# Eight fused layers on one core: the order of 1,112 steps from a table in place of a rule of turns

## The chip, the core and the metric

One core of a Trainium2 chip runs the whole program in one launch. Five instruction streams run side by side: TensorE (PE, with its weight loads PEld), VectorE (DVE), ScalarE (ACT), GpSimd (POOL) and SyncE (SP, which only issues DMAs here). Each executes its own instructions strictly in the order in which the program writes them, and they meet at semaphores. The metric is the device time of one execution in microseconds.

## The reference

A batch of 8 sequences of 256 tokens, 128 wide, goes through four attention layers and four feed-forward layers in turn. Each adds to `x` (arguments abridged, comments added):

```python
x = x + _L0_xattn_ref(_layernorm(x), ctx_1024, ...)  # L0x: gated retention, 16 heads
x = x + _L0_ffn_ref(_layernorm(x), ...)              # L0f: 8 experts, top 2, GELU
x = x + _L1_xattn_ref(_layernorm(x), ctx_1024, ...)  # L1x: bidirectional attention flow
x = x + _L1_ffn_ref(_layernorm(x), ...)              # L1f: shared + 7 experts, top 1, SwiGLU
x = x + _L2_xattn_ref(_layernorm(x), ctx_1024, ...)  # L2x: 16 heads, masked softmax
x = x + _L2_ffn_ref(_layernorm(x), ...)              # L2f: quantised, with a width-3 convolution
x = x + _L3_xattn_ref(ctx_1024, _layernorm(x), ...)  # L3x: 8 heads, 512 keys, normed q and k
x = x + _L3_ffn_ref(_layernorm(x), ...)              # L3f: 2 groups of 32 experts, top 2, SwiGLU
```

The mixture layers (L0f, L1f, L3f) choose experts by token, so rows are sent to DRAM by expert, read back in blocks, multiplied, stored and fetched again.

## The kernel before, in words

`x` stays in on-chip memory. Every layer is cut into units over the batch: L0x 4, L0f 2, L1x 8, L1f 2, L2x 8, L2f 8, L3x 8, L3f 4. A unit of a layer needs only the same tokens of the layer before, so units of neighbouring layers overlap, at most two of one layer. A unit is written as up to six generators (`on_pe`, `on_dve`, `on_act`, `on_pool`, `on_sync`), one an engine, each cut by `yield` into the same number of steps. L2x.5.11 below means layer L2x, unit 5, step 11 (counted from 0). One step of a unit stands on every engine at the same place of the list of steps; `stepwise` walks that list once for each engine and lets the generator of that unit emit its next piece. So the list alone sets the order of work inside every in-order stream. A "+L1x" entry is the place at which SP issues the weight loads of a layer.

The list has 1,112 entries. In the kernel before it is made by `tensor_program`, a rule of turns: the active units take turns in the order of layers; each time round a unit gains the credit of its layer in `STEPS` (0.8 to 1.7) and gives a step for each whole credit; a unit starts when the layer before has finished its tokens and the memory slabs that it needs are free (`SLABS`), and the second unit of a layer keeps a distance to the first.

Steps that the prediction speaks of, with the lines of the profile:

- L0f: `turn`, `up`, `down` of an expert block, one each step from step 15 on (L786, L795, L804, L806), GELU on ACT (L903), DVE copies (L850). L1x.0: transposes of the normed tokens (L362) and first product (L1426). `normalise` (L249 to L282) is a layer norm on DVE, `moments` (L303, L306) only its statistics, with the root on POOL (L315 to L332).
- L2x: steps 5 to 8 give scores to PSUM, which DVE reduces (L1791); steps 11 and 13 transpose the maxima (L1676), steps 14 to 18 are scores again and products (L1702, L1689), Exp on ACT (L1858); step 0 of a unit projects the context (L1628 to L1638).
- L2f: steps 5 to 8 are three matmuls each (L1972, L1974, L1976), with SiLU on ACT (L2103); step 10 transposes (L1987), DVE quantises (L2068 to L2075), and step 12 transposes its result (L1996).
- L3x: DVE step 0 is `moments` (with the one-time `set_up`, L2338 to L2343, in unit 0), step 2 writes the normed tokens (L2377), PE transposes them in step 3 (L2201); step 11 waits on DVE for key and query norms whose roots POOL makes (L2523, then L249 to L267) and scales (L2356); steps 15 to 18 turn heads and give scores, of which DVE takes maxima to step 22 (L2399); steps 24 to 32 are scores and products (PE L2272, Exp on ACT L2498, L2502), step 36 is the output product (L2325), after which DVE norms it.
- L3f: DVE step 0 is `normalise` of 4 tiles; steps 17 to 30 are 12 chunks, one a step: transposes of rows (L2711), up (L2734), down (L2747), SiLU on ACT (L2944), a DVE product (L2883); rows come by SP (L2615, stores L2623, weights L2633).

PSUM banks are given out in a ring of eight by `Banks.take` in the order of PE's steps; the next taker waits until the reader of the last use is done.

Of the kernel before, what the change touches and what calls it, by code (L numbers as in the profile page):

```python
# [146 lines left out]
def build(nc, ins, out):  # L147
    ctx = ExitStack()
    with ctx:
# [2855 lines left out]

        def tensor_program():

            uses = {n: set("".join(SLABS[n])) | set("" if n[1] == "3" else "G") for n in LAYERS}  # L3010
            started, finished, asked = dict.fromkeys(LAYERS, 0), dict.fromkeys(LAYERS, 0), []
            given = dict.fromkeys(LAYERS, 0)
            active, order = [], []
            ahead, apart = {(n, u): 0 for n in LAYERS for u in range(UNITS[n])}, {}

            def vacant(name, slabs):
                return not any(uses[n] & set(slabs) and finished[n] < UNITS[n] for n in LAYERS[:LAYERS.index(name)])

            def ask():
                while len(asked) < len(LAYERS) and vacant(LAYERS[len(asked)], SLABS[LAYERS[len(asked)]][0]):  # L3020
                    order.append(("load", LAYERS[len(asked)]))
                    asked.append(LAYERS[len(asked)])

            def start():
                for k, n in reversed(list(enumerate(LAYERS))):
                    mine = [a for a in active if a[1] == n]
                    if (n in asked and started[n] < UNITS[n] and len(mine) < 2
                            and vacant(n, SLABS[n][1] + (SLABS[n][2] if started[n] else ""))
                            and all(a[2] for a in mine)
                            and (k == 0 or given[LAYERS[k - 1]] * UNITS[n]  # L3030
                                 >= (started[n] + 1) * UNITS[LAYERS[k - 1]] * PARTS[LAYERS[k - 1]])):
                        active.append([made[n][1](started[n]), n, False, 0.0, started[n]])
                        started[n] += 1
                        return True
                return False

            ask()
            while start() or active:
                active.sort(key=lambda a: LAYERS.index(a[1]))
                for entry in list(active):  # L3040
                    unit, n, second, _, u = entry
                    before = next((a for a in active if a[1] == n and a[4] < u), None)
                    if second and entry is not next(a for a in active if a[1] == n):
                        continue
                    entry[3] += STEPS[n]
                    while entry[3] > 0.999:
                        if before in active and ahead[n, u - 1] - ahead[n, u] < apart[n]:
                            entry[3] = 0.0
                            break
                        if entry[2] and not vacant(n, SLABS[n][2]):  # L3050
                            break
# [182 lines left out]
```

## Time and profile before

| | us |
|---|---|
| median of three runs | 1491.45 (1487.0 to 1491.95) |
| span of the profiled execution | 1483.4 |
| PE busy in that span | 1185.0 (80%) |
| DVE, ACT, POOL busy | 802.1, 673.0, 433.6 |

The profile gives the profiled execution's time as its span, from the first instruction to the last. Nothing else of its own time is recorded, and the runs' median is 8.05 us above the span. A row's idle time stands before the named instruction, with what released it. PEclk is the share of full clock granted to PE.

### The profile page before, as it was taken

How to read it: one execution, taken by the hardware profiler on the slowest of the kernel's cores; microseconds unless marked ns; L12 is line 12 of the kernel's file. 1: busy time of each engine (PE TensorE's matmuls, PEld its weight loads, DVE VectorE, ACT ScalarE, POOL GpSimd, SP SyncE). 2: the span in 40 equal slices, each digit the busy share in tenths (PEclk: the TensorE clock that was granted, in tenths of full speed). 3: DMA queues.
4: the chain of work that ended last, by engine and by line, in shares of the span. 5: the costliest groups of instructions: out<-in, count | busy, mean ns of one | idle time of the engine just before them, and what ended most of it. 6: DMA issues, size and time to landing. Idle time of an engine off the chain costs nothing. (4 is left out here: it accounts for less than half of the span.)

```text
span 1483.4 us, 28125 instructions
## 1 busy us (share of the span) xinstructions
PE 1185.0 (80%) x10844; PEld 919.1 (62%) x10844; DVE 802.1 (54%) x2259; ACT 673.0 (45%) x1373; POOL 433.6 (29%) x822
## 2 busy tenths in 40 slices
PE   6776865987876899876878968969988997899453
PEld 4555865875875678554545755747764776578343
DVE  6676304436646345577557456485358535761722
ACT  1222544752442554543554735534754475447121
POOL 2214232005412311223261221216051515142234
PEclk9887997988996999898988989989997999899777
DMA  9002874535530324200000270004520452055165
GB/s 270 3 2 94 250 259 130 173 108 175 182 107 4 125 91 144 74 1 1 1 1 1 108 237 0 4 6 132 144 66 10 137 141 59 11 161 143 29 205 165
DMA packets 141144, 146.62 MB, mean 99 GB/s; under 512 B 13395, under 2 KB 125011, under 8 KB 140371
## 3 DMA queue, kind: packets, MB, share of 16 engines
q1 hardware_dynamic: 133842, 130.13, 28.6%
q0 software_dynamic: 7168, 14.69, 3.1%
q8 instruction: 86, 1.41, 0.4%
q14 instruction: 48, 0.39, 0.1%
HBM read 107.69 MB, written 37.09 MB: 98 GB/s over the span
## 5 line engine op out<-in xcount | busy, mean ns | idle before, releaser
L315 POOL TENSOR_SCALAR rsq_v<-moment 128x2 f32<-128x2 f32 (+1 forms) x26 | 6.2, 239 | 322.7 <-DVE moment L306 319.1
L2964 POOL DMA_INDIRECT L3f_rows<-xn,slabG x64 | 63.6, 993 | 119.6 <-DVE slabG L2841 101.7
L2399 DVE TENSOR_REDUCE slabB<-bank 128x1 f32<-128x512 f32 x128 | 78.6, 680 | 8.5 <-PE bank L2244 8.5
L1791 DVE TENSOR_REDUCE slabA<-bank 128x2 f32<-128x512 f32 x128 | 78.4, 682 | 4.1 <-PE bank L1663 4.0
L2883 DVE TENSOR_TENSOR slabG<-bank,slabG 128x256 f32<-128x256 f32 x48 | 20.2, 422 | 108.2 <-ACT slabG L2944 108.2
L1858 ACT ACTIVATE slabE<-bank 128x512 f32<-128x512 f32 x112 | 58.0, 618 | 34.9 <-PE bank L1702 34.7
L2272 PE MATMUL bank<-slabB,slabW 128*128 128x128 f32 x512 | 69.7, 281 | 0.0
L2383 DVE TENSOR_REDUCE slabW<-slabC 128x8 f32<-128x512 f32 x48 | 32.4, 680 | 65.9 <-ACT slabC L2462 65.8
L1074 POOL DMA_INDIRECT slabA<-L0f_made,slabA x32 | 30.8, 961 | 123.9 <-DMA L0f_made<-slabA 114.8
L2272 PEld LDWEIGHTS bank<-slabB,slabW 128*128 128x128 f32 x512 | 61.9, 192 | 8.2 <-issue 7.8
L903 ACT ACTIVATE slabA<-bank,slabA 128x128 f32<-128x128 f32 x184 | 52.7, 375 | 22.6 <-PE bank L795 21.7
L1702 PE MATMUL bank<-slabA 32*128 32x256 f32 x512 | 48.4, 448 | 13.2 <-DVE slabC L2071 10.0
L1226 PE MATMUL bank<-slabC,slabB 128*128 128x128 f32 x448 | 56.5, 281 | 1.6 <-ACT slabC L1351 1.2
L795 PE MATMUL bank<-slabA 128*128 128x128 f32 x368 | 52.5, 289 | 5.0 <-DMA slabA<-e_w_dram 3.7
L2211 PE MATMUL bank<-slabB,slabW 128*128 128x512 f32 x96 | 56.1, 670 | 0.4 <-DVE slabA L1801 0.3
L2462 ACT ACTIVATE slabC<-bank 128x512 f32<-128x512 f32 x48 | 28.8, 601 | 59.4 <-PE bank L2211 44.7
L1226 PEld LDWEIGHTS bank<-slabC,slabB 128*128 128x128 f32 x448 | 53.9, 197 | 2.5 <-ACT slabC L1351 1.7
L850 DVE COPY slabA<-bank 128x128 f32<-128x128 f32 x46 | 13.3, 290 | 73.8 <-PE bank L806 53.4
L2931 ACT ACTIVATE slabG<-bank 128x512 f32<-128x512 f32 x48 | 29.0, 604 | 52.6 <-PE bank L2711 52.4
L795 PEld LDWEIGHTS bank<-slabA 128*128 128x128 f32 x368 | 48.4, 205 | 7.2 <-issue 6.5
L2980 POOL DMA_INDIRECT slabC<-L3f_made,slabG x32 | 30.6, 957 | 70.4 <-DMA L3f_made<-slabC 61.7
L2711 PE MATMUL bank<-ident,slabE 128*128 128x128 f32 x192 | 31.5, 290 | 23.4 <-DMA slabE<-L3f_rows 23.4
(469 smaller groups left out, 3382.3 us busy)
## 6 DMA issues: line engine op xcount, KB each, us to landing
slabA<-e_w_dram SPq DMA_DIRECT2D x46, 578.0 KB, 4.3
slabB<-e_w_dram SPq DMA_DIRECT2D x28, 768.0 KB, 4.4
slabE<-L3f_rows SPq DMA_DIRECT2D x48, 256.0 KB, 3.5
L3f_made<-slabC SPq DMA_DIRECT2D x48, 256.0 KB, 2.5
slabD<-e_w_dram SPq DMA_DIRECT2D x64, 128.0 KB
ctxT<-e_w_dram SPq DMA_DIRECT2D x64, 128.0 KB
L3f_rows<-slabG SPq DMA_DIRECT2D x4, 1536.0 KB, 18.3
L0f_rows<-slabG SPq DMA_DIRECT2D x2, 1472.0 KB, 10.2
```

Source lines behind the costliest of these rows:

```text
L795: m = T.matmul(k.ap[:, tile_cols(c)], w1(n, c), rowsT[n % 2], start=True, stop=True, skip_group_check=True)
L903: A.activation(hb[n % 2][:, tile_cols(c)], k.ap[:, tile_cols(c)], ACT.Gelu, bias=b1(n, c)).then_inc(*(act.tell(*k.read) if c == FB - 1 els ...
L1226: m = T.matmul(k.ap[:, tile_cols(c)], w[:, j, tile_cols(c)], rowsT[n % 2], start=True, stop=True, skip_group_check=True)
L1702: m = T.matmul(bs[j].ap[:, kt * S:(kt + 1) * S], z["KT"][r, c, tile_cols(kt)], z["QT"][r, c, :], start=True, stop=True, skip_group_check=True)
L1791: V.tensor_reduce(nmx[:, :, c, 32 * j + HD:32 * j + HD + 1], b.ap.rearrange("p (i s) -> p i s", i=2), AX.X, ALU.max, negate=True).then_inc ...
L1858: A.activation(probs[(4 * c + j) % 8], b.ap, ACT.Exp).then_inc(*act.tell(*b.read))
L2211: T.matmul(b.ap, kvT[:, tok], Wk if kind == "kn" else Wq, start=True, stop=True, skip_group_check=True).then_inc(b.full[0])
L2272: m = T.matmul(obs[i].ap[:, tile_cols(h % 4)], p.ap[:, j * S + i * P:j * S + (i + 1) * P], Vv[:, ((2 * half + j) * H + h) * (HD + 1):((2 * ...
L2383: V.reduce_sum(norms[:, 8 * n:8 * n + 8], by_head(sqs[n % 2]), AX.X).then_inc(*dve.tell(sem("l3x_norms"), 6 * u + n + 1))
L2399: V.tensor_reduce(nmx[:, i, 64 * e + k:64 * e + k + 1], b.ap, AX.X, ALU.max, negate=True).then_inc(*dve.tell(*b.read))
L2711: t = T.transpose(b.ap[:, tile_cols(j)], rowsb[m % 3][:, j, :], ident)
L2964: G.indirect_dma_start(sent[u % 2][r], bass.IndirectOffsetOnAxis(ap=to[u % 2][:, k, 2 * t + r:2 * t + r + 1].bitcast(U32), axis=0), xn[:, ...
```

## The change

The credits, the slab rules and the rule of turns are gone. `TURNS`, a table written out by hand or by a program, lists the same 1,112 entries in another order; `turns` unpacks it and `tensor_program` only walks it. No instruction is added, removed or resized in the source. Of the 1,104 steps, 232 stand at the same place among the steps as before, 829 have moved by up to ten places and 43 by 11 to 17. The first 38 steps and the last ones from the last L3x unit's end (all of L3f.3) stand as before. The loads move too: +L1x from entry 2 to 11, +L1f 78 to 87, +L2x 212 to 220, +L2f 213 to 242, +L3x 384 to 383, +L3f 617 to 630. Line numbers after the table are 48 higher.

```diff
+TURNS = """
++L0x +L0f L0x.0*8 L0x.1 +L1x L0x.0 L0x.1 L0x.0 L0x.1 L0x.0 L0x.1 L0x.0 L0x.1 L0x.0 L0x.1 L0x.0 L0x.1 L0x.0
...
-        SLABS = {"L0x": ("B", "CE", ""), "L0f": ("A", "", ""), "L1x": ("", "E", ""), "L1f": ("B", "CD", ""),
-                 "L2x": ("A", "AE", ""), "L2f": ("", "CD", ""), "L3x": ("BW", "", ""), "L3f": ("A", "GCDE", "")}
-        STEPS = {"L0x": 1, "L0f": 1, "L1x": 1, "L1f": 1.15, "L2x": 1.7, "L2f": 1.4, "L3x": 1.08, "L3f": 0.8}
+        def turns(table):
+            steps = []
+            for entry in table.split():
+                step, _, times = entry.partition("*")
+                name, _, u = step.partition(".")
+                steps += [("load", name[1:]) if name[0] == "+" else (name, int(u))] * int(times or 1)
+            return steps
         def tensor_program():
...
-            while start() or active:
-                active.sort(key=lambda a: LAYERS.index(a[1]))
-                for entry in list(active):
...
+            units = {}
+            for n, u in order:
+                if n == "load":
+                    continue
+                if (n, u) not in units:
+                    units[n, u] = made[n][1](u)
+                next(units[n, u], "end")
...
-        order = tensor_program()
+        order = turns(TURNS)
+        tensor_program()
```

Three places show what the table moves. Each is given as the rows of one engine's stream, merged when equal rows follow each other.

First place, PE at the start of unit 0 of L1x, whose transposes are L362 and whose first product is L1426; L786 to L806 are expert blocks of L0f. Before:

```order
L786 MATMUL bank<-ident,slabA 128x128
L362 MATMUL bank<-ident,xn 128x128 x2
L786 MATMUL bank<-ident,slabA 128x128
L795 MATMUL bank<-slabA 128x128 x4
L1426 MATMUL bank<-ctxT,slabE 128x256 x2
L1432 MATMUL bank<-slabG,xnT 128x1 x2
L786 MATMUL bank<-ident,slabA 128x128
L795 MATMUL bank<-slabA 128x128 x4
```

The same place with the table (L410 is L362, L1474 is L1426):

```order
L834 MATMUL bank<-ident,slabA 128x128 x2
L843 MATMUL bank<-slabA 128x128 x4
L834 MATMUL bank<-ident,slabA 128x128
L843 MATMUL bank<-slabA 128x128 x4
L852 MATMUL bank<-slabA,ones 128x128
L854 MATMUL bank<-slabA 128x128 x4
L834 MATMUL bank<-ident,slabA 128x128
L843 MATMUL bank<-slabA 128x128 x4
L852 MATMUL bank<-slabA,ones 128x128
L854 MATMUL bank<-slabA 128x128 x4
```

and, after one more such block,

```order
L852 MATMUL bank<-slabA,ones 128x128
L854 MATMUL bank<-slabA 128x128 x4
L410 MATMUL bank<-ident,xn 128x128 x2
L1474 MATMUL bank<-ctxT,slabE 128x256 x2
L1480 MATMUL bank<-slabG,xnT 128x1 x2
```

Four steps of L0f.1 (16 to 19) have moved ahead of L1x.0's transposes and first product; before, one step stood between the two.

Second place, DVE where L3x begins: the set-up of L3x (L2338 to L2343) and the reductions of L2x.5 (L1791). Before:

```order
L1791 TENSOR_REDUCE slabA<-bank 128x2 x8
L2338 TENSOR_SCALAR slabW<-slabW 128x16
L2339 TENSOR_SCALAR slabW<-slabW 128x1
L2341 MEMSET slabB 128x256
L2343 MEMSET slabB 128x2144 x2
L303 BN_STATS stats<-ctxt 128x6 x2
L303 BN_STATS stats<-x 128x6 x2
L306 BN_AGGR moment<-stats 128x2 x4
L376 TENSOR_TENSOR x<-bank,x 128x256
L1791 TENSOR_REDUCE slabA<-bank 128x2 x4
```

With the table (L1839 is L1791, L1849 the copy of the transposed maxima, L2386 to L2391 the set-up):

```order
L424 TENSOR_TENSOR x<-bank,x 128x256
L1839 TENSOR_REDUCE slabA<-bank 128x2 x4
L1849 TENSOR_TENSOR slabA<-bank,slabA 128x512 x2
L351 BN_STATS stats<-x 128x6 x2
L354 BN_AGGR moment<-stats 128x2 x2
L2386 TENSOR_SCALAR slabW<-slabW 128x16
L2387 TENSOR_SCALAR slabW<-slabW 128x1
L2389 MEMSET slabB 128x256
L2391 MEMSET slabB 128x2144 x2
L351 BN_STATS stats<-ctxt 128x6 x2
```

The last four reductions of L2x.5 and both copies now stand ahead of the set-up.

Third place, DVE where L3f.1's layer norm meets L3x.5: L282 is the end of that norm, L2399 the maxima of L3x.4, L2377 the normed tokens of L3x.5. Before:

```order
L260 SCALAR_TENSOR_TENSOR rsq_y<-rsq_t,rsq_y 128x4
L282 TENSOR_SCALAR xn<-x,meanvar,rsq_y 128x128 x4
L2368 TENSOR_SCALAR slabD<-slabW 128x256
L2399 TENSOR_REDUCE slabB<-bank 128x1 x4
L2377 TENSOR_SCALAR slabW<-ctxt,moment,slabW 128x128 x2
L2377 TENSOR_SCALAR slabW<-x,moment,slabW 128x128 x2
L2896 SCALAR_TENSOR_TENSOR x<-slabC,slabG,x 128x128 x8
```

With the table (L2425 is L2377, L2447 is L2399, L2431 a later sum of L3x.5, L321 the start of L3f.1's norm, L2931 and L2910 belong to L3f.0):

```order
L2931 TENSOR_TENSOR slabG<-bank,slabG 128x256
L2447 TENSOR_REDUCE slabB<-bank 128x1 x4
L2425 TENSOR_SCALAR slabW<-ctxt,moment,slabW 128x128 x2
L2425 TENSOR_SCALAR slabW<-x,moment,slabW 128x128 x2
L2931 TENSOR_TENSOR slabG<-bank,slabG 128x256
L2910 COPY slabC<-bank 128x512
L2944 SCALAR_TENSOR_TENSOR x<-slabC,slabG,x 128x128 x8
L2447 TENSOR_REDUCE slabB<-bank 128x1 x12
L2431 TENSOR_REDUCE slabW<-slabC 128x8
L321 BN_STATS stats<-x 128x6 x4
L324 BN_AGGR meanvar<-stats 128x2 x4
```

L3f.1's norm has moved behind L3x.5's normed tokens, and the products of five late chunks of L3f.0 (steps 26 to 30) stand around them. The ACT stream also changes in one kind of instruction: the compiler puts a table load (ACT_TABLE_LOAD) where the function on ACT changes between sets, and with the table it puts 73 instead of 107.

## Rows read from the trace of the kernel before

**Rows 1.** The page: busy us, share of the span, instructions, by engine.

```profile
PE 1185.0 (80%) x10844; PEld 919.1 (62%) x10844; DVE 802.1 (54%) x2259; ACT 673.0 (45%) x1373; POOL 433.6 (29%) x822
```

**Rows 2.** Stretches A:B: length, busy (count) of PE PEld DVE ACT POOL, PEclk, DMA.

```profile
85.00:1384.00 1299.00, 1085.17 (x9437) 843.67 (x9429) 707.85 (x2006) 635.38 (x1305) 380.70 (x742) 0.91 0.30 94
1040.00:1100.00 60.00, 59.62 (x707) 45.46 (x703) 21.89 (x40) 43.20 (x73) 16.03 (x26) 1.00 0.42 116
1106.00:1117.00 11.00, 1.81 (x16) 1.05 (x16) 10.20 (x43) 0.01 (x1) 6.04 (x18) 0.72 0.08 25
1117.00:1128.00 11.00, 10.72 (x35) 5.38 (x36) 10.05 (x21) 3.19 (x6) 0.00 (x0) 0.50 0.00 0
```

**Rows 3.** What PE waited for: total us, times, longest.

```profile
PE bank L2201 <- DVE slabW L2377: 31.7, 6, 9.3
PE bank L804 <- ACT slabA L903: 5.4, 5, 1.4
```

**Rows 4.** Timeline of PE about L1x.0: start, us, instruction, [idle before].

```profile
234.43 0.66 PE L362 MATMUL bank<-ident,xn 128*128 128x128 f32 x2 [8.60 <-DVE xn L282]
239.60 2.05 PE L1426 MATMUL bank<-ctxT,slabE 128*128 128x256 f32 x4 [2.58 <-DVE slabE L1500]
242.15 0.46 PE L786 MATMUL bank<-ident,slabA 128*128 128x128 f32 x1
245.10 0.61 PE L1440 MATMUL bank<-ident,slabE 128*128 128x128 f32 x4
```

**Rows 5.** Timeline about L2x.5.11, DVE and PE.

```profile
688.84 0.16 DVE L2338 TENSOR_SCALAR slabW<-slabW 128x16 f32<-128x16 uint8 x1
695.21 0.39 DVE L376 TENSOR_TENSOR x<-bank,x 128x256 f32<-128x256 f32 x1
698.14 1.09 PE L1676 MATMUL bank<-ident,slabA 128*128 128x128 f32 x4 [7.76 <-DVE slabA L1791]
```

**Rows 6.** Timeline about L2x.6.16, POOL, DVE and PE.

```profile
750.57 0.22 POOL L315 TENSOR_SCALAR rsq_v<-moment 128x2 f32<-128x2 f32 x1 [26.50 <-DVE moment L306]
756.24 0.33 POOL L2523 TENSOR_SCALAR rsq_v<-slabW 128x48 f32<-128x48 f32 x1 [0.16 <-POOL xn L332]
761.11 3.59 DVE L2356 TENSOR_TENSOR slabB<-slabB,slabW 128x512 f32<-128x512 f32 x3 [10.69 <-POOL slabW L267]
768.49 2.08 PE L1702 MATMUL bank<-slabA 32*128 32x256 f32 x14 [6.25 <-DVE slabC L2071]
```

**Rows 7.** Timeline of PE about L2f.5.12 and L2f.6.4.

```profile
867.10 0.60 PE L1972 MATMUL bank<-slabD,slabC 128*128 128x256 f32 x2
868.39 1.95 PE L2325 MATMUL bank<-slabB,xn 128*128 128x128 f32 x16
878.02 0.59 PE L1996 MATMUL bank<-identb,slabD 128*128 128x128 bf16 x4 [7.24 <-DVE slabD L2075]
886.98 0.66 PE L1964 MATMUL bank<-ident,slabC 128*128 128x128 f32 x2 [2.97 <-DVE slabC L2054]
```

**Rows 8.** Timeline about L3x.5.3, DVE and PE.

```profile
1108.66 0.87 DVE L273 BATCH_NORM_STATS2 stats<-x 128x6 f32<-128x128 f32 x4
1113.19 0.28 DVE L2368 TENSOR_SCALAR slabD<-slabW 128x256 bf16<-128x256 uint8 x1
1117.04 1.09 PE L2201 MATMUL bank<-ident,slabW 128*128 128x128 f32 x4 [9.16 <-DVE slabW L2377]
```

**Rows 9.** Timeline of PE in the last unit, L3f alone.

```profile
1436.52 0.66 PE L2711 MATMUL bank<-ident,slabE 128*128 128x128 f32 x4
1439.20 0.66 PE L2711 MATMUL bank<-ident,slabE 128*128 128x128 f32 x4
1442.89 0.66 PE L2711 MATMUL bank<-ident,slabE 128*128 128x128 f32 x4 [0.92 <-DMA slabE<-L3f_rows]
```

**Rows 10.** Groups of ACT: line, operation xcount | busy us, mean ns | idle before.

```profile
L2944 ACT ACT_TABLE_LOAD x19 | 24.4, 1283 | 0.3
```

**Rows 11.** The page: a DMA issue, KB each, us from issue to landing.

```profile
slabE<-L3f_rows SPq DMA_DIRECT2D x48, 256.0 KB, 3.5
```

More of the change, by code:

```diff
@@ new lines @@
+L1x.6 L1f.0 L1x.5 L1x.6 L1f.0 L1x.5 L1x.6 +L2f L1f.0 L1x.6 L1f.0 L1x.6 L1x.7 L1f.0*3 L1x.6 L1x.7 L1f.0*4 L1x.6
+L1x.7 L1x.6 L1x.7*3 L1f.0 L1x.7*3 L2x.0 L1f.0*2 L1f.1 L2x.0 L1f.1 L2x.0 L1f.1*3 L2x.0*5 L1f.1 L2x.0 L1f.1*3
+L2x.0*4 L2x.1 L2x.0 L1f.1 L2x.0 L2x.1*2 L2x.0*2 L2x.1*2 L2x.0 L2x.1 L1f.1 L2x.0*2 L1f.1*2 L2x.1 L1f.1 L2x.1
+L2x.0 L1f.1 L2x.0 L2x.1*2 L1f.1 L2x.0 L2x.1 L2x.0 L1f.1 L2x.1*3 L1f.1 L2x.1 L1f.1*2 L2x.2 L2x.1 L1f.1*2 L2x.1
+L2x.2*2 L2x.1 L2x.2*2 L2x.1*2 L2x.2 L1f.1 L2x.1*2 L2x.2 L1f.1 L2x.2 L2x.1 L1f.1 L2x.2 L1f.1*2 L2x.2 L2x.1
@@ new lines @@
+L3x.1 L3x.0 L2f.3 L2f.4 L2f.3 L3x.1 L2x.7 L3x.0 L3x.1 L3x.0 L2x.7*2 L3x.0 L2f.4*2 L2f.3 L2x.7*2 L2f.4 L2f.3*2
+L2x.7 L2f.4 L2x.7 L2f.4*6 L3x.1 L3x.0 L3x.1 L2f.5 L2f.4 L3x.0*2 L2f.4 L2f.5 L3x.0*2 L2f.4 L2f.5 +L3f L2f.5
+L3x.0*2 L2f.4 L3x.0*5 L2f.5 L2f.4*2 L2f.5*5 L3x.1*3 L3x.2 L2f.5*2 L2f.6 L2f.5*2 L2f.6 L2f.5 L2f.6 L3x.1 L3x.2
+L3x.1 L3x.2 L2f.6 L2f.5 L2f.6 L2f.5 L3x.1 L3x.2 L2f.5 L2f.6*2 L3x.1 L3x.2 L3x.1 L3x.2 L2f.6*3 L3x.1 L3x.2 L3x.1
+L2f.6*2 L3x.2 L3x.1 L2f.7 L3x.2 L2f.6 L3x.1 L2f.6 L2f.7 L3x.2 L3x.1 L2f.6 L3x.1 L3x.2 L2f.7 L3x.1 L2f.7 L2f.6
@@ L28 @@
+"""
 class Lane:
@@ L2998, in build @@
                 "L2f": bitnet(), "L3x": attention8(), "L3f": moe_small()}
-        SLABS = {"L0x": ("B", "CE", ""), "L0f": ("A", "", ""), "L1x": ("", "E", ""), "L1f": ("B", "CD", ""),
-                 "L2x": ("A", "AE", ""), "L2f": ("", "CD", ""), "L3x": ("BW", "", ""), "L3f": ("A", "GCDE", "")}
-        STEPS = {"L0x": 1, "L0f": 1, "L1x": 1, "L1f": 1.15, "L2x": 1.7, "L2f": 1.4, "L3x": 1.08, "L3f": 0.8}
-        def tensor_program():
[L3010 to L3037, printed above, removed]
-            while start() or active:
-                active.sort(key=lambda a: LAYERS.index(a[1]))
-                for entry in list(active):
[L3041 to L3051, printed above, removed]
-                        entry[3] -= 1
-                        order.append((n, u))
-                        ahead[n, u] += 1
-                        v = next(unit, "end")
-                        if v == "end":
-                            active.remove(entry)
-                            finished[n] += 1
-                            given[n] += 1
-                            ask()
-                        elif v == "part":
-                            given[n] += 1
-                        elif v == "next":
-                            entry[2] = True
-                            apart[n] = ahead[n, u]
-                        if v:
-                            break
-            return order
@@ new lines, in turns @@
+        def turns(table):
[5 more added lines that the diff above has]
+            return steps
+        def tensor_program():
+            units = {}
[5 more added lines that the diff above has]
+                next(units[n, u], "end")
+            assert all(next(unit, "end") == "end" for unit in units.values())
```

33 lines of the change are left out of this document (added).

## The prediction

> **What bounds the kernel now.** I read four views. The page comes first: PE is busy for 80% of the span, no other engine for more than 54% [rows 1]. The reader is to see that PE carries the time and that the rest of the span is PE waiting. Second come the stretches. Before 85 us and after 1384 us the table leaves almost everything in place, so all that can change lies between. There PE is busy 1085.17 of 1299 us, so it stands idle for 213.8 us, and its granted clock is 0.91 on average, a mix of 2.4 GHz (1.00) and 1.2 GHz (0.50) [rows 2]. That idle time and the half-speed time behind it are all there is to win. Where L3x and L3f run side by side (1040 to 1100) there is nothing: 59.62 of 60 us busy at clock 1.00 [rows 2]. Third comes the list of what PE waited for. The longest sums come from DVE: six waits on L3x's normed tokens cost 31.7 us, the longest 9.3 [rows 3]. Fourth, the timeline around the long waits shows each time the same picture: PE stands at the head of its stream on one semaphore, its releaser is in DVE's or POOL's stream behind a long piece of another unit, and PE has independent work further down which it may not take, since each stream is in order. Such waits are a matter of the order alone, and the order is what changes.
>
> **The change part by part.** Every instruction of PE, DVE and POOL stays, so their busy times stay at equal clock. I work out the places where PE's long waits are.
>
> L1x.0. PE waits 8.60 us for the transposes and 2.58 us for the first product; between the two stands one step of L0f.1 [rows 4]. With the table L0f.1's steps 16 to 19 stand ahead of both. A step of that kind lasts 2.95 us there (242.15 to 245.10) [rows 4], partly at half clock. One of the four was already between the waits, and step 16 lacks its `down`: about 7.5 of the 11.2 us get filled. The DVE copies of these blocks follow L0f.0's late sum, but eight PSUM banks at three a block let nearly three blocks through. The end that excludes most is 3 us (bank ring full at once), the other 11.2; I take 7.5.
>
> L2x.5.11. PE waits 7.76 us for the last maxima of L2x.5. DVE did L3x's set-up, its first moments and a late sum first, from 688.84 to 695.21: 6.3 us [rows 5]. In the new order they come behind. What is late next is L3x.0.3, which needs the moments; L2x.5's steps 13 and 14 and L2x.6.0 now stand ahead of it. Gain 6.3, between 3 and 7.8.
>
> L2x.6.16. PE waits 6.25 us, since DVE stood 10.69 us on the roots of L3x.0.11. POOL made them from 756.24, because L2f.3.0's layer norm stood in front from 750.57, and that itself had waited for DVE [rows 6]. The table puts L3x.0.11 ahead of L2f.3.0, so POOL's queue loses 5.7 us in front of the roots (750.57 to 756.24). L2f.3.0's own norm is needed only some ten steps later. Gain 5.5, between 2 and 6.2.
>
> L2f.5.12 and L2f.6.4. PE waits 7.24 and 2.97 us for quantised values: DVE layer-norms L3x.0's output first, and PE has nothing between its last product and the wait [rows 7]. With the table L3x.0.36 comes earlier, and L2f.5's four triples of matmuls stand between: a triple takes 1.29 us (867.10 to 868.39) [rows 7], four of them 5.2, with some transposes 7.1. The second wait gets 10 us of PE work where it had under 3. Gain 9.5 of 10.2; at least 5.
>
> L3x.5.3. PE waits 9.16 us. DVE had L3f.1's layer norm in front of the normed tokens, from 1108.66 to 1113.19, 4.5 us [rows 8]; the norm now follows. Also five chunks of L3f.0 stand about this place, a whole chunk being 2.68 us [rows 9] and the last two shorter, some 10.7 us of PE work. Gain 8.5, between 4.5 and 9.2. What hides them is a stretch in which DVE is busy 10.20 of 11 us [rows 2], so their own DVE products are paid there, a little over 2 us, which I have taken off in the next paragraph. The twins at L3x.3.3 and L3x.7.3 (two of the six waits, the longest 9.3 [rows 3]) keep the norm of L3f in front: no gain.
>
> These five give 7.5 + 6.3 + 5.5 + 9.5 + 8.5 = 37.3 us. The rest of the idle time is 213.8 less their waits of 44.6: 169.2 us. For about forty waits over 1.2 us I followed the releasers back to a PE instruction and added up PE's own work that stands between the two in each order. It grew at 16, shrank at 7 and stayed at the others. The ends are a loss of 15% of the 169.2 (25 us) and a gain of 25% (42). I take +10 us net, which includes the waits that the moves newly make and the 2 us from above.
>
> The ACT stream loses 34 of 107 table loads of 1283 ns [rows 10], 43.6 us of its 673.0. ACT is not the bound [rows 1]: it is hidden beside PE's matmuls, and the largest wait of PE on a function of this kind sums to 5.4 us [rows 3]. I count 0 for it beyond the +10; the ends are 0 and 12. The Trainium skill (ScalarE: Activation LUTs, Rules for kernel authors) says to budget about 2.7 us for every switch. By that figure ACT would lose 92 us and not 43.6; the trace says 1.283, and at either price the sum above is the same.
>
> The loads of weights stand 8 to 29 entries later or at their place, and no wait on them is among PE's long ones; nothing, unless a first matmul comes too soon after: between 0 and -5.
>
> A cost stands against it. Before, chunks of L3f alternated with score steps of L3x, and rows came by DMA meanwhile. Now some 30 of the 36 chunks of L3f.0 to L3f.2 follow each other with little between. The last unit shows such a chain: a chunk takes 2.68 us (1436.52 to 1439.20) when rows are there, and 3.69 (to 1442.89) when not [rows 9]. Between 0 and 1.01 us each; I take 0.25, nearer to the first since rows are prefetched two chunks ahead: 30 x 0.25 = 8 us.
>
> Idle time sum: 37.3 + 10 - 8 = 39 us. The clock comes on top: behind the 9.16 us wait PE was granted 0.50 for 11 us, in which it was busy 10.72 [rows 2]; half of it, 5.4 us, is lost, 0.59 us for each us of waiting. Over 85 to 1384 the mean of 0.91 gives at most 0.09 x 1085 = 98 us for 213.8 us idle, 0.46; short waits cost less. I take 0.3: 39 x 1.3 = 51 us. The profiled span is 1483.4; 1483.4 - 51 = 1432.4. The median of the runs lies 8.05 us above that span, which I carry over: 1440.5, so **1441 us**.
>
> **The rivals.** Waits move instead of closing. DVE is busy 10.20 of 11 us in the stretch before L3x.5.3 [rows 2]; whatever stands first there, the last piece is as late. For it: the twins stay, and seven followed waits got less cover. Against it: over the whole span DVE is busy 54% [rows 1], so its work can go beside PE-heavy steps. Half of the 37.3 and the low end for the rest: 18.6 - 8 - 8 = 3 to 10 us, with the clock 1478 to 1488; I name 1481.
>
> More than forecast. The five waits close wholly, 44.6, the rest gives 20%, 34, no cost at L3f: 79 x 1.3 = 102, so 1389. For it: long waits with a cover that now exceeds them twice over; against it: the DMA waits and the two twins cannot close.
>
> Slower: L3f's rows starve in the long rows of chunks. SP's one queue issues rows, stores and weights of L3f in order, and a load of rows takes 3.5 us to land [rows 11]; three buffers hold them. If the loads come no longer ahead, a chunk costs up to 3.5 us more. The point from which it decides is 51/30 = 1.7 us a chunk, besides what I have counted; at 2.2 us the 30 chunks cost 66 in place of 8, and the time is 1441 + 58 = 1499. Against it speaks the tail, where the largest spacing in such a chain is 1.01 us above the best [rows 9], with one unit alone. The stretch at 1040 to 1100, fully busy with the two layers mixed [rows 2], speaks for leaving them mixed. The Trainium skill (Perfetto Trace Analysis, Optimization Strategy) says that regimes with different most-contended engines may gain by being interleaved; the table takes apart two layers there, which this rule speaks against, and at five chunks of L3f.0 it mixes them better into DVE's stretch.
>
> The order doesn't matter: PE's waits would be set by chains through DMA and POOL that no order shortens, and the time stays at 1491. Against it: the five waits above all had DVE or POOL work of another unit in front.
>
> **How the numbers follow.** Forecast 0.62, with its own range 1418 to 1462. More than forecast 0.12 (around 1389 to 1410). Waits move 0.15, most of it faster, a fifth of it within the bound. Slower by starving 0.07. Order without effect 0.04, of which a fourth counts as slower or faster. A measurement of this kernel can tell about 0.3%, 4.5 us, from no change. Faster: 0.62 + 0.12 + 0.12 + 0.01 = 0.87. Same: 0.03 + 0.02 = 0.05. Slower: 0.07 + 0.01 = 0.08. The range leaves out the strongest gains and the slower cases: 1400 to 1480.
>
> **What would show it.** In the changed profile PE's busy time falls by 10 to 20 us through the clock alone, and its idle time from 298 to about 260. The waits at L1x.0, L2x.5.11, L2x.6.16, L2f.5.12 and L3x.5.3 are under 2 us each, L3x.3.3 and L3x.7.3 near 9. ACT has 73 table loads and 43.6 us less. PE's wait for L3f's rows before the last unit is under 10 us in sum. I am wrong if PE's idle time stays near 298, if DVE waits at the same five places for something else, or if L2711 waits on rows come up among the first three of PE's waits outside the tail.

## The result, and the profile after

| | before | after |
|---|---|---|
| median of the runs, us | 1489.23 (4 runs) | 1434.25 (4 runs, 1425.99 to 1435.96) |
| span of the profiled execution | 1483.4 | 1431.7 |
| PE busy / idle in it | 1185.0 / 298.4 | 1165.6 / 266.1 |
| ACT table loads | 107 | 73 |

The ratio is 0.9617, 95% interval 0.9596 to 0.9639: faster by 55 us, where 1441, 48 us less than this median, was forecast. The profiled execution took 1432.98 us for a span of 1431.7: 1.3 us lie around the span, and 1.25 to 1.43 in every later run.

The page after, which answers to [rows 1]:

```profile
span 1431.7 us, 28123 instructions
PE 1165.6 (81%) x10844; PEld 908.1 (63%) x10844; DVE 795.5 (56%) x2259; ACT 632.7 (44%) x1339; POOL 430.3 (30%) x822
```

PE's idle time fell by 32.3 us and its busy time by 19.4 with the same 10,844 matmuls; together they are the 51.7 us of the span. The mean granted clock rose from 0.893 to 0.909, and busy time times clock is nearly the same in both (1058 and 1060 us), so, as far as a mean over the span can tell, the 19.4 us are clock and not work. ACT lost 34 instructions and 40.3 us. The stretches after, columns as in [rows 2]. The first is the part that can change; it now ends at 1332, where it ended at 1384:

```profile
85.00:1332.00 1247.00, 1064.02 (x9387) 831.84 (x9385) 702.53 (x2011) 595.07 (x1271) 382.51 (x747) 0.92 0.32 98
1228.60:1326.50 97.90, 90.16 (x1090) 73.55 (x1089) 41.88 (x103) 43.96 (x85) 39.15 (x49) 0.97 0.45 130
```

213.8 us of idle time became 183.0 there. The second is a loss; in the trace before, the same 60 steps (entries 998 to 1057) take

```profile
1290.40:1379.90 89.50, 87.99 (x1091) 71.16 (x1089) 34.05 (x78) 54.05 (x93) 30.69 (x40) 1.00 0.46 135
```

so a stretch with 1.5 us of idle time at clock 1.00 became one with 7.7 at 0.97. What PE waited for, after, which answers to [rows 3] (total, times, longest):

```profile
PE bank L2759 <- DMA slabE<-L3f_rows: 29.9, 11, 20.6
PE bank L2249 <- DVE slabW L2425: 11.7, 3, 9.3
PE bank L1474 <- DVE slabE L1548: 9.6, 4, 6.7
PE bank L852 <- ACT slabA L951: 1.4, 2, 0.9
```

The waits on L3x's normed tokens fell from 31.7 to 11.7 us. Of the rows of L3f (first line) 20.6 is the one in the last unit, before its first chunk.

The five places, in the order of [rows 4] to [rows 8], PE's timeline with the idle time before an instruction in brackets. L1x.0, and DVE beside it:

```profile
234.68 0.38 PE L410 MATMUL bank<-ident,xn 128*128 128x128 f32 x2
241.74 2.05 PE L1474 MATMUL bank<-ctxT,slabE 128*128 128x256 f32 x4 [6.68 <-DVE slabE L1548]
248.11 1.09 PE L1497 MATMUL bank<-ident,slabE 128*128 128x128 f32 x4 [1.99 <-DVE slabE L1565]
```

```profile
238.37 2.31 DVE L913 SCALAR_TENSOR_TENSOR x<-slabA,x 128x128 f32<-128x128 f32 x8 [4.19 <-DMA slabA<-L0f_made,slabA]
241.19 0.40 DVE L1548 TENSOR_SCALAR slabE<-xnT,slabG 128x256 f32<-128x256 f32 x1
```

The wait for the transposes is gone, the one for the first product is 6.68 in place of 2.58: DVE stands at L0f.0's late sum until its gathered rows land at 238.4, whatever PE does meanwhile. Then L2x.5.11, L2x.6.16 and what follows it, L2f.5.12 and L2f.6.4, L3x.5.3, and the twin L3x.7.3:

```profile
685.35 1.04 PE L1724 MATMUL bank<-ident,slabA 128*128 128x128 f32 x8
740.53 1.55 PE L1750 MATMUL bank<-slabA 32*128 32x256 f32 x16
746.80 0.44 PE L410 MATMUL bank<-ident,xn 128*128 128x128 f32 x2 [3.71 <-POOL xn L380]
843.06 0.59 PE L2044 MATMUL bank<-identb,slabD 128*128 128x128 bf16 x4 [2.95 <-DVE slabD L2123]
851.93 0.44 PE L2012 MATMUL bank<-ident,slabC 128*128 128x128 f32 x2 [2.30 <-DVE slabC L2102]
1056.42 0.66 PE L2249 MATMUL bank<-ident,slabW 128*128 128x128 f32 x4
1207.67 1.09 PE L2249 MATMUL bank<-ident,slabW 128*128 128x128 f32 x4 [9.31 <-DVE slabW L2425]
```

Lines without a bracket had no wait: L2x.5.11 (7.76 before), L2x.6.16 (6.25) and L3x.5.3 (9.16). Behind L2x.6.16 a wait of 3.71 us on POOL's norm for L2x.7 is new: L2f.3.0's norm, which the table took away from in front of L3x.0.11's roots, now stands directly in front of it (POOL):

```profile
735.26 0.22 POOL L363 TENSOR_SCALAR rsq_v<-moment 128x2 f32<-128x2 f32 x1 [5.59 <-DVE moment L354]
740.93 0.50 POOL L363 TENSOR_SCALAR rsq_v<-moment 128x2 f32<-128x2 f32 x1 [0.18 <-POOL xn L380]
```

The longest new wait stands at a place that the prediction does not name, L2x.3.5, on a piece of POOL that waits for DVE, behind eight gathers of L1f:

```profile
604.56 0.62 PE L1711 MATMUL bank<-slabA 32*128 32x256 bf16 x8 [6.55 <-POOL slabA L1936]
```

Entries 255 to 384, in which it lies, take about as long as before (183.1 us and 182.5), since other waits there closed.

**The two traces lined up.** Both orders have run the same set of steps at many entries. The end of the last PE matmul of that set gives a time in each trace, and the difference of two such times is what a stretch took, however its steps are ordered. us, PE idle in brackets:

| entries | holds | before | after | change |
|---|---|---|---|---|
| 128-152 | L1x.0 | 54.8 (25.7) | 54.7 (23.5) | -0.2 (-2.1) |
| 448-482 | L2x.5.11 | 37.0 (10.2) | 27.8 (3.7) | -9.2 (-6.4) |
| 522-538 | L2x.6.16 | 26.7 (8.4) | 18.2 (4.7) | -8.5 (-3.7) |
| 632-708 | L2f.5.12, L2f.6.4 | 75.7 (17.0) | 64.2 (8.0) | -11.4 (-8.9) |
| 815-876 | L3x.5.3 | 79.5 (12.4) | 70.3 (5.7) | -9.2 (-6.7) |
| 877-997 | | 153.6 (16.0) | 153.4 (19.1) | -0.2 (+3.1) |
| 998-1057 | | 89.4 (1.5) | 97.9 (7.7) | +8.4 (+6.2) |
| 1058-1111 | end | 82.6 (40.5) | 85.9 (42.1) | +3.3 (+1.6) |

The five places give 38.5 us, all the rest up to entry 877 some 23, and what follows takes 11.5 back; the last 1.6 stand behind the last matmul. Most of the 23 lie in entries 543 to 631 (8.8), 709 to 814 (7.9) and 385 to 447 (4.0); no run tests one of these alone.

### The profile page after: what moved, and what is told of

Its sections match the earlier page's. It is cut to its first block and busy times, and to the rows that moved or that the text cites. A ratio compares the mean times of both kernels' runs of the same rounds, so it can differ in the third digit from the quotient of the medians.

```text
span 1431.7 us, 28123 instructions
## 1 busy us (share of the span) xinstructions
PE 1165.6 (81%) x10844; PEld 908.1 (63%) x10844; DVE 795.5 (56%) x2259; ACT 632.7 (44%) x1339; POOL 430.3 (30%) x822
## 5 line engine op out<-in xcount | busy, mean ns | idle before, releaser
L2447 DVE TENSOR_REDUCE slabB<-bank 128x1 f32<-128x512 f32 x128 | 78.7, 682 | 10.7 <-PE bank L2292 10.7
L1839 DVE TENSOR_REDUCE slabA<-bank 128x2 f32<-128x512 f32 x128 | 78.6, 684 | 3.4 <-PE bank L1711 3.2
L2931 DVE TENSOR_TENSOR slabG<-bank,slabG 128x256 f32<-128x256 f32 x48 | 20.3, 424 | 87.2 <-ACT slabG L2992 87.2
L843 PE MATMUL bank<-slabA 128*128 128x128 f32 x368 | 53.8, 293 | 6.4 <-DMA slabA<-e_w_dram 6.1
L2259 PE MATMUL bank<-slabB,slabW 128*128 128x512 f32 x96 | 51.8, 622 | 0.1
L1115 POOL DMA_INDIRECT L0f_rows<-xn,slabA x32 | 31.2, 976 | 66.2 <-DVE slabA L1096 57.1
L854 PE MATMUL bank<-slabA 128*128 128x128 f32 x368 | 50.0, 280 | 0.0
L2431 DVE TENSOR_REDUCE slabW<-slabC 128x8 f32<-128x512 f32 x48 | 32.1, 679 | 31.5 <-ACT slabC L2510 31.3
```

The source lines that it names most:

```text
L843: m = T.matmul(k.ap[:, tile_cols(c)], w1(n, c), rowsT[n % 2], start=True, stop=True, skip_group_check=True)
L854: m = T.matmul(k.ap[:, 0:P], hb[n % 2][:, tile_cols(c)], w2(n, c), start=False, stop=c == FB - 1, skip_group_check=True)
L1839: V.tensor_reduce(nmx[:, :, c, 32 * j + HD:32 * j + HD + 1], b.ap.rearrange("p (i s) -> p i s", i=2), AX.X, ALU.max, negate=True).then_inc ...
L2259: T.matmul(b.ap, kvT[:, tok], Wk if kind == "kn" else Wq, start=True, stop=True, skip_group_check=True).then_inc(b.full[0])
L2431: V.reduce_sum(norms[:, 8 * n:8 * n + 8], by_head(sqs[n % 2]), AX.X).then_inc(*dve.tell(sem("l3x_norms"), 6 * u + n + 1))
L2447: V.tensor_reduce(nmx[:, i, 64 * e + k:64 * e + k + 1], b.ap, AX.X, ALU.max, negate=True).then_inc(*dve.tell(*b.read))
```

## The experiments

Each run is compared with runs of the kernel before on its own chip. The first four ran on one chip (before: 1490.28), without the new kernel beside them: their mark is its 0.9617 of the first comparison, whose chip the record does not name (before: 1489.23). Both are called the first chip here. The next four and the last four ran on two others, each with the new kernel beside them.

**e1, the middle alone.** The old order, and between the two marks the new:

```
 entries    0..384   as before
+entries  385..876   as in the new table
 entries  877..1111  as before
```

> The old order, with entries 385 to 876 alone taken from the new table (L2f.0.0 to L3f.1.6; both orders have run the same steps at either end of this stretch). Theory: the gain is PE waits closed by independent steps in between, so it is additive by place, and the two traces, lined up at places where the same steps are done, give 59.5 us of it to this stretch and losses of 8 behind it. The time is then about 1489 - 59 = 1430 us, as good as the new table or a little better (1425 to 1436). Rival one, the gain comes from the 34 ACT table loads that are gone: 16 of the 34 are gone in this stretch, so about half of the gain, 1462. Rival two, waits move: the old order behind the stretch was fitted to nothing in it and takes back a part, 1440 to 1455.

Measured: 1440.56 us, ratio 0.9675 (0.9651 to 0.9699). The stretch took 468.7 us in place of 520.3, 51.6 of the 59.5 us. What is missing in it is mostly clock (385 to 482: idle 14.4, against 12.8 with the new table and 23.0 before, but PE busy 82.7 against 75.3). Behind the stretch comes a wait that my cut made, and entries 877 to 997 took 161.2 us, where they took 153.6 before:

```profile
1092.73 0.42 PE L2748 MATMUL bank<-slabG 128*128 128x320 bf16 x1 [6.46 <-DVE slabG L2848]
```

L3f.1.7 now follows L3f.1.6 at once, and DVE has yet to choose the experts; either whole order has steps in between. The gain lies where the traces put it. The first rival (1462) is refuted; the time alone would also fit the low end of the second, but the only long wait that is new behind the stretch is the one at the seam.

**e2, entries 998 to 1057 as before.**

```
 entries    0..997   as in the new table
+entries  998..1057  as before
 entries 1058..1111  as in the new table
```

> The new table, with entries 998 to 1057 alone (60 of 1112: L3x.6's and L3x.7's score steps and L3f.2's chunks) in the old order. In the traces this stretch lasted 97.9 us with the new order and 89.4 with the old. Theory (order alone, additive): 8 us less than the new kernel, 1426 us, ratio to the kernel before about 0.956. If the rival holds that table loads cost time, it gets slower: 8 of the 34 loads come back, 10 us of ACT, 1440 to 1444. If the 8 us were only the state of the clock in that execution, no change, 1434.

Measured: 1437.43, ratio 0.9654 (0.9627 to 0.9681), not the 0.956 expected. The stretch took 95.7 us, where the new order took 97.9 and 89.4 were expected. The order of these 60 steps makes up 2.2 of the 8.5 us at most; the wait at L3x.6.34 stays (3.55 us). The new kernel's trace shows it (POOL, DVE, PE):

```profile
1233.58 1.01 POOL L3012 DMA_INDIRECT L3f_rows<-xn,slabG  x1 [19.82 <-DVE slabG L2889]
1243.57 0.34 POOL L2571 TENSOR_SCALAR rsq_v<-slabW 128x48 f32<-128x48 f32 x1
```

```profile
1248.52 2.14 DVE L2404 TENSOR_TENSOR xnT<-xnT,slabW 128x512 f32<-128x512 f32 x2 [8.83 <-POOL slabW L315]
```

```profile
1252.91 1.33 PE L2364 MATMUL bank<-ident,xn 128*128 128x128 f32 x5 [3.54 <-DVE xn L2463]
```

POOL's eight scatters of L3f.2.8 (10 us) start late and run ahead of L3x.7.11's roots; DVE stands 8.83 us on those, with L3x.6's division behind them. It is a matter of what the streams carry into the stretch, so the table above says where time was lost, not which entries lost it.

**e3, one move undone.**

```
+L3x.0.0        ahead of L2x.5.8
+L3x.0.1        ahead of L2x.5.10
+L3x.0.2        ahead of L2x.5.11
-L3x.0.0 to .2  behind L2x.6.0 (new table)
```

> The new table, with L3x.0's first three steps alone moved back ahead of L2x.5.8, L2x.5.10 and L2x.5.11, as the old order has them; all else as in the new one. Theory: DVE's set-up and moments of L3x.0 stand again in front of L2x.5's last maxima, PE waits some 6.3 us there, with the clock 8: 1442 us, and the trace shows the wait at L2x.5.11 again. Rival, waits move: what DVE does early it need not do late, and a later wait shrinks by as much: 1434 to 1436.

Measured: 1442.94, ratio 0.968 (0.9651 to 0.9708), 8.7 us more. The wait is back:

```profile
698.48 1.09 PE L1722 MATMUL bank<-ident,slabA 128*128 128x128 f32 x4 [5.78 <-DVE slabA L1837]
```

In the span it is 8.3 us, 3.9 of them idle and 4.4 clock; entries 385 to 482 took 98.4 us, 88.1 in the new kernel. That a wait on DVE is cured by the order alone is shown here, and the number of table loads is 73 in both; the rival gave no change.

**e4, the table loads put back.**

```
+                    if u < 3 and i % 2:
+                        A.activation(spare, b.ap[:, 0:1], ACT.Exp).then_inc(*act.step())
                     A.activation(hs[m % 2], b.ap[:, 0:256], ACT.Silu).then_inc(*act.tell(sem("l3f_silu"), m + 1))
```

> The new kernel, with one more activation of a single column by Exp ahead of the Silu of every second chunk in L3f.0 to L3f.2, 18 of them; each makes ACT switch its table there and back, so up to 36 table loads of 1283 ns come back, 46 us of ACT, about as many as the new order saved, and where it saved many of them. Theory: ACT is hidden, 0 to 12 us, so 1434 to 1446. Rival, the gain is the table loads: 1434 + 46 and more, 1480 or above.

It has 105 table loads, 32 more than the new kernel, most in two groups:

```profile
L2995 ACT ACT_TABLE_LOAD x22 | 28.2, 1283 | 0.4
L2994 ACT ACT_TABLE_LOAD x16 | 20.5, 1283 | 0.3
```

Measured: 1449.5, ratio 0.9721 (0.9697 to 0.9745): 15 us more for 41 us of ACT, and 3.5 above the range expected. In the stretches that were changed it is 1.3 + 5.2 + 3.2 = 9.7 us, 0.3 us a load; the rest stands in stretches with the same instructions and nearly the same idle time (118 to 254: 226.5 us against 220.0; e2 has 226.6 there), so it is the clock of the execution. The rival, that the loads are the gain (46 us and more), is refuted; my 0 for them was low. The 34 loads saved would be 10 of the 55 us at 0.3 us a load, and 16 at the 0.48 that the medians give (15.25 us for 32). The traces before and after say less: in entries 877 to 997 ten loads went and the time moved by 0.2, while entries 448 to 482 went from one load to two and 522 to 538 had none in either order, and these two gave 17.7 us.

**e5, the new kernel on a second chip.**

> The new kernel once more, unchanged, as the mark for the other runs: ratio to the kernel before 0.962, and the same waits at the same places. What differs between its two traces is what an execution adds by itself.

Measured: 1540.82 against 1566.95, ratio 0.9833 (0.9799 to 0.9866). The expectation failed: the gain is less than half of that on the first chip; see the section on the hardware. Waits of single places can still be read in these traces, differences in the time of a few us hardly.

**e6, the norm behind L3x.7.3.**

```
-L3f.2.0 L3x.7.2 L3x.6.19 L3x.7.3
+        L3x.7.2 L3x.6.19 L3x.7.3 L3f.2.0
```

> The new table with one step moved: L3f.2.0 (DVE's layer norm of 4.7 us for L3f.2) from in front of L3x.7.2 to behind L3x.7.3, the place where the prediction said that both orders leave a wait of 9 us (9.3 in the new trace). Theory: DVE can norm L3x's tokens as soon as POOL's roots are there (1203.4 in the new trace) and 1.1 us later PE goes on, so the wait falls to about 6.2, and with the clock the time by 4 to 5 us: 1430. Rival, waits move: L3f.2.3 then waits for the norm, no change.

Measured: 1545.41, ratio 0.9855 (0.9832 to 0.9878), not faster than e5's 0.9833.

```profile
1291.00 1.09 PE L2247 MATMUL bank<-ident,slabW 128*128 128x128 f32 x4 [6.35 <-DVE slabW L2423]
1298.82 2.08 PE L2257 MATMUL bank<-slabB,slabW 128*128 128x512 f32 x2 [4.06 <-DVE slabB L2445]
```

The wait fell from 9.3 to 6.35, as worked out (6.2), but the 4 to 5 us of time did not come: L3x.7.5 now waits 4.06 us for maxima that the norm is ahead of. The waits move here, though not to L3f.2.3, as the rival had it.

**e7, the norm back in front of L3x.5.2.**

```
+L3f.1.0 L3x.5.2 ... L3x.5.3 L3x.4.20 ... L3x.5.5
-        L3x.5.2 ... L3x.5.3 L3x.4.20 ... L3x.5.5 L3f.1.0
```

> The new table with one step moved back: L3f.1.0 (the norm of L3f.1) in front of L3x.5.2, as the old order has it; the five chunks of L3f.0 stay about L3x.5.3. It tells the two reasons apart that the prediction gave for the wait of 9.2 us gone there. If the norm in DVE's stream is what counts: DVE is 4.7 us later for L3x.5.2 and the chunk's product behind it, PE waits 4 to 5 us more, 1438 to 1441. If the chunks as cover suffice: less than 1 us, 1434 to 1435.

Measured: 1541.64, ratio 0.9845 (0.9816 to 0.9875): in the time undecided against e5. The aligned stretch decides: entries 815 to 879 took 85.0 us, against 78.6 in e5 and 79.9 in e6 and e8, which have the new order there. In the trace (PE, then DVE):

```profile
1128.01 1.97 PE L2793 MATMUL bank<-ctxT,slabG 64*64 64x128 f32 x16 [6.21 <-DVE slabG L2929]
```

```profile
1121.98 0.87 DVE L319 BATCH_NORM_STATS2 stats<-x 128x6 f32<-128x128 f32 x4
1126.51 0.59 DVE L2423 TENSOR_SCALAR slabW<-ctxt,moment,slabW 128x128 f32<-128x128 f32 x2
1127.54 0.41 DVE L2929 TENSOR_TENSOR slabG<-bank,slabG 128x256 f32<-128x256 f32 x1
```

The chunk's last product waits 6.21 us in place of 1.5, the 4.7 us of the norm, and L3x.5.3 still does not wait. So the chunks are the cover and the norm behind them is what lets the chunks run: at L3x.5.3 the cover without the other half is not enough. The norm behind without the cover was tried at L3x.7.3 alone (e6).

**e8, four more places mended.**

```
+L0f.0.47 L0f.0.48   behind L1x.0.2
+L3f.0.0 to .2       behind L3x.3.3;  L3f.0.3 behind L3x.3.7;  L3x.3.0 ahead of L2f.7.13
+L3f.2.0             behind L3x.7.3;  L3x.7.0 ahead of L3x.5.36
+L3f.2.8             behind L3x.7.11
```

> The new table with four more places mended by the same rule (nothing in front of a piece that PE waits for, of another unit and not yet due). L0f.0.47 and .48 (a sum on DVE that waits for POOL's gather) behind L1x.0.2; L3f.0.0 to .2 behind L3x.3.3, L3f.0.3 behind L3x.3.7, and L3x.3.0 ahead of L2f.7.13; L3f.2.0 behind L3x.7.3, and L3x.7.0 ahead of L3x.5.36; L3f.2.8 (eight indirect DMAs on POOL, 10 us) behind L3x.7.11, whose roots stood behind it. Theory: of the waits 6.7 + 2.0, 5.0 + 1.8, 9.3 and 3.5 us in the new trace, 28.3 together, some 20 go, with the clock 28 to 32 us: 1402 to 1408. Rival, waits move: what stood in front is now itself late (the sum for L1x.1, the routing of L3f.0, the rows of L3f.2), half of it comes back: 1418 to 1425. Other rival: the sorted rows of L3f.2 come so late that its chunks wait for them: 1434 or more.

Measured: 1551.67, ratio 0.9897 (0.987 to 0.9924), slower than the new kernel beside it (0.9833) and far from the 1402 to 1408 expected. With the scatter behind the roots the wait at L3x.6.34 is gone, but the rows are late, as the other rival said:

```profile
1348.69 1.11 PE L2758 MATMUL bank<-ident,slabE 128*128 128x128 f32 x4 [9.17 <-DMA slabE<-L3f_rows]
```

and the two others of L3x moved on: 5.0 + 1.8 became 2.8 + 4.6, 9.3 became 3.2 + 3.8. At L1x.0 there was little to cure on this chip (1.0 + 2.5 in e5). The rule "nothing undue in front" alone does not make a better order.

**e9 and e10, the five places alone.** e9 is the new kernel on a third chip.

> The new kernel unchanged, as the mark for the three beside it on the same chip. In the call before, both kernels ran 5 to 7% longer on another chip (1567 and 1541 us) and PE paused inside runs of matmuls; whether this chip does that decides how the others are read: 1434 and ratio 0.962 if not, about 1541 and 0.983 if it does.

e10, the old order with the new one at five stretches:

```
+entries 128..152, 448..482, 522..538, 632..708, 815..879  as in the new table
 all others                                                as before
```

> The old order with the new one at the five places of the prediction alone (entries 128 to 152, 448 to 482, 522 to 538, 632 to 708, 815 to 879; both orders have run the same steps at each end). The prediction gave these places 37.3 us of waits and with the clock 48 us: 1441. The two traces, lined up at those ends, give 38.5 us (0.2, 9.2, 8.5, 11.4 and 9.2): 1451, ratio 0.974. If waits move on to where the old order follows: 1465 to 1475. If the gain comes from elsewhere (table loads, the other moves): above 1475.

Measured: before 1577.86; e9 1542.91, ratio 0.9778 (0.9746 to 0.981); e10 1544.0, ratio 0.9783 (0.9758 to 0.9809). On this chip the old order with the five stretches gives 34 of the 35 us. The kernel before was not traced here, so the stretches are compared with e9 and not with their old lengths. The third was not tested: the step that decides it, L3x.0.11 ahead of L2f.3.0, stands at entry 517, outside my cut, and the stretch kept 27.3 us. The others came as in the new kernel: 28.1, 64.1 and 73.1 us (27.7, 64.9 and 71.8 in e9). What the new table gives besides (543 to 631: 74.2 us against e10's 83.7) it loses elsewhere (998 to 1057: 113.7 against 103.2; 153 to 254: 178.7 against 173.6). So three places carry this run: L2x.5.11, L2f.5.12 with L2f.6.4, and L3x.5.3, since L1x.0's stretch gave only 0.2 us on the first chip. The sum is not closed for the first chip, where the other moves are worth some 13 us net (51.7 less 38.5).

**e11, chunks as cover at L3x.7.3.**

```
-L3f.1.26 ... L3f.1.30 among L3x.5.19 to L3x.5.26;  L3f.2.0 ahead of L3x.7.2
+L3f.1.26 ... L3f.1.30 among L3x.7.0 to L3x.7.2;    L3f.2.0 behind L3x.7.5
```

> The new table with 35 entries about L3x.7.3 in another order: the last five chunks of L3f.1 (L3f.1.26 to .30, with what follows them) stand about L3x.7.0 to L3x.7.2 as cover, and L3f.2.0 (the norm) behind L3x.7.5, after the pattern that the new order has at L3x.5.3. The run with the norm alone behind showed that the wait moves two steps on, to maxima that DVE has still to take; this one gives PE 10 us of its own work there. Theory: the wait of 9.3 us goes and none of over 3 us takes its place, 10 to 14 us less than the new kernel on the same chip, 1420 to 1424 (0.953). Rival: the chunks were needed where they stood (L3x.5.19 to .25 waits for ACT and DVE instead), 1430 to 1436. Other rival: L3f.1's late gather holds up POOL, DVE and the rows of L3f.2, 1440 or more.

Measured: 1538.39, ratio 0.9753 (0.9728 to 0.9777); e9 has 0.9778. The 9.3 us are gone and entries 877 to 997 took 163.8 us in place of 170.1, but two waits are new in the place of the chunks and at the cover, the first over the 3 us that I had said none would pass:

```profile
1254.76 1.97 PE L2362 MATMUL bank<-ident,xn 128*128 128x128 f32 x8 [4.20 <-DVE xn L2461]
1275.50 1.09 PE L2793 MATMUL bank<-ctxT,slabG 64*64 64x128 f32 x16 [1.59 <-DVE slabG L2929]
```

4.5 us less in the medians, where 10 to 14 were expected; the two intervals overlap, and it wasn't tried on the first chip. It may beat both kernels, and this does not show it.

**e12, the late sum behind L1x.0.2.**

```
-L0f.0.47 L0f.0.48 L0f.1.15 ... L1x.0.2
+                  L0f.1.15 ... L1x.0.2 L0f.0.47 L0f.0.48
```

> The new table with L0f.0.47 and .48 alone moved behind L1x.0.2. It asks why L1x.0 gained so little (the waits there are 6.7 + 2.0 us in the new trace, where the prediction left 3.7): DVE stood in L0f.0.47, a sum of gathered rows, until 238.4, since POOL gathers until 235.3, and the piece for L1x.0.3 is behind it. Theory: the order of DVE's stream, so the wait at L1x.0.3 falls from 6.7 to about 1 and the time by 6 to 9 us, 1426 to 1428. Rival: the sum is itself needed at once (L1x.1.0 normalises what it writes) and the wait moves to L1x.1's first matmuls: 1432 to 1436.

Measured: 1545.61, ratio 0.9794 (0.9764 to 0.9823): no gain, and no answer. On this chip the wait that it should cure is 1.0 us in e9 too, because chunk L0f.1.18 waits 6.0 us for ACT first. Why L1x.0 gained so little on the first chip rests on the DVE row above alone.

## Why the prediction was right, by its steps

The mechanism was right: waits of PE on pieces that stood behind another unit's work in DVE's or POOL's stream, closed by order. e3 shows it for one place by undoing it, e10 for three without the rest of the table.

- **The five places: 37.3 us of idle time predicted, 27.8 measured** in the aligned stretches. L2x.5.11 gave 6.4 (6.3), L2f.5.12 with L2f.6.4 8.9 (9.5), L3x.5.3 6.7 (8.5), L2x.6.16 3.7 (5.5; 3.71 us reappeared at L2x.7.2), L1x.0 2.1 (7.5). The step that failed is the last: I filled PE's wait with chunks and did not ask when DVE is free again. Its late sum waits for the gathered rows until 238.4, and PE's wait ends behind it (the row of DVE above; no run tested it). "Under 2 us each" held at three places of five.
- **The rest of the idle time: +10 net predicted**; up to entry 877 it was 14.4 (42.2 in entries 118 to 876 less 27.8), of which entries 709 to 814 gave 7.4 and 385 to 447 gave 3.8. The loads of weights cost nothing where they moved first: entries 0 to 117 took 211.3 us in both.
- **Chunks of L3f in rows: -8 predicted, -10.9 measured** (idle in entries 877 to 1111), but not by the way of the sum. The rows cost 1.5 and 2.4 us before the last unit; more come from DVE's divisions for L3x (3.5 and 2.5 us), the first behind POOL's scatter, and e2 shows of the first that the order of the steps around it is not what sets it.
- **Idle in sum: 39 predicted, 32.3 measured**, and PE's busy time fell by 19.4, where 10 to 20 was said. ACT has the 73 table loads forecast and 40.3 us less, where 43.6 was said.
- **The clock: 0.3 us for each us of idle time predicted, 0.60 measured** (19.4 for 32.3). The rows had it: 0.59 behind the one long wait, 0.46 as a bound on the mean. I discounted for short waits, but the waits that closed were the long ones. This term was 7.7 us low, the idle sum 6.7 high; they cancel, so 51 against 51.7 is partly luck.
- **ACT's table loads: 0 predicted**, between 0 and 10 by e4's stretches, which is inside the ends given, and 16 by its medians, which is not.
- **What lies around the span: 8.05 us predicted, 1.25 to 1.43 in every run with both numbers.** So the profiled execution before took about 1484.7 us, less than any run timed (1487.0): the median of the runs was no offset to its span. With 1.3 the forecast would have been 1433.7.
- **The rivals.** "Waits move" was wrong for the whole and right for places: L2x.7.2, and in e6 and e8 wherever only the obstacle was moved and no cover brought. "L3f's rows starve" did not come (its sum before the last unit is 4.4 us, under the 10 said), but e8 shows 9.17 us of it when the scatter is held back. Of the twins, L3x.7.3 stayed as predicted (9.31). L3x.3.3 did not: its own wait fell from 9.33 to 1.80, behind a new one of 4.97 at L3f.0.3. Two sums of the rivals were wrong as written: "waits move" takes a loss of 8 as the low end for the rest, where the end given earlier was 25, and with 25 it is a slower kernel; the 1.7 us a chunk at which starving decides divides 51 us with clock by the chunks, and by idle time it is 39/30 = 1.3.

The rule on interleaving that I weighed from the Trainium skill (Perfetto Trace Analysis, Optimization Strategy) spoke for leaving L3x and L3f mixed. No run here shows it: after entry 877, where the table takes the two apart, idle time rose by 10.9 us, but e2 mixed entries 998 to 1057 again as before and got back 2.2 of the 8.5 us there. At L3x.5.3, where the table brings chunks into DVE's stretch, the rule and the gain agree.

## What to carry to other kernels

In programs of in-order streams, look for PE at the head of its stream waiting on a piece that stands behind another unit's long piece; mend it by bringing PE work that is ready (cover) and moving the obstacle behind what the cover needs, both at once, since the obstacle alone moved the wait two steps on (e6) and the cover alone waited itself (e7). Both together are no guarantee: in e11 they closed 9.3 us and opened 4.20 and 1.59 where the cover came from and where it went. Before counting a cover, find when the releasing engine is itself free: at L1x.0 it stood behind a DMA. And price idle time with the clock behind it, here 0.59 us for each us of one long wait and 0.60 over the whole span.
